# Two groups of a float32 graph product side by side, and a first half-tile rounded on VectorE

## The reference

```
h   = maximum((x - mean(x)) / sqrt(var(x) + 1e-5), 0)     # x: 4096 x 256, by row
agg = adj @ h                                             # adj: 4096 x 4096
out = x + maximum(agg @ W.T + b, 0)                       # W: 256 x 256
```

## Time and profile before

| What | Value |
|---|---|
| Time before | 380.95 us, median of 3 runs (380.69 to 380.96) |
| The profiled execution's own time | 380.8 us |
| Its span | 379.0 us |
| TensorE busy | 375.1 us, 99% of the span, 1651 matmuls |
| VectorE, ScalarE, GpSimd busy | 212.2, 181.8 and 50.1 us |
| Chain that ended last | TensorE 98% of it |
| Moved by DMA | 80.25 MB, mean 212 GB/s |

### The profile page before, as it was taken

The page is one execution under the profiler, slowest core; times in us unless marked ns, Lnnn a source line. Parts: engine busy times, 40 slices in busy tenths (PEclk is TensorE's granted clock), DMA queues, the critical chain, the costliest instruction groups (busy, mean ns, idle before and its releaser), DMA issues.

```text
span 379.0 us, 4516 instructions
## 1 busy us (share of the span) xinstructions
PE 375.1 (99%) x1651; PEld 308.1 (81%) x1651; DVE 212.2 (56%) x294; ACT 181.8 (48%) x228; POOL 50.1 (13%) x88
## 2 busy tenths in 40 slices
PE   8999999999999999999999999999999999999997
PEld 4888888888888888888888888888888888888885
DVE  5999988874744453535564544444464444444424
ACT  5888776764443434343643343433355243434341
POOL 5687732320010000000001000000000100000000
PEclk9999999999999999999999999999999999999999
DMA  7989877577659565655566856565656775555203
GB/s 263 369 301 304 275 256 258 185 235 256 210 186 317 174 215 178 208 177 209 176 206 207 294 178 209 178 205 184 201 189 195 256 242 195 187 202 185 92 2 111
DMA packets 22774, 80.25 MB, mean 212 GB/s; under 512 B 2496, under 2 KB 2880, under 8 KB 22752
## 3 DMA queue, kind: packets, MB, share of 16 engines
q1 hardware_dynamic: 19584, 68.30, 54.1%
q0 software_dynamic: 3168, 11.67, 8.6%
HBM read 75.76 MB, written 4.19 MB: 211 GB/s over the span
## 4 chain that ended last, share of the span: by engine, by line
PE 98%; DMA 1%; DVE 0%; ACT 0%; POOL 0%; issue 0%; POOLq 0%
PE bank L421 92%; PE bank L463 6%; DMA x_sb<-x_dram 1%; ACT adj_hi L346 0%; POOL rstd L204 0%; ACT h_sb L352 0%; DVE out_sb L320 0%; DVE stats L240 0%; DVE mean_var L245 0%; DVE var_eps L249 0%; POOLq L200 0%
## 5 line engine op out<-in xcount | busy, mean ns | idle before, releaser
L421 PE MATMUL bank<-adj_hi,h_sb 128*128 128x512 f32 x1024 | 254.3, 389 | 0.2 <-ACT adj_hi L346 0.2
L229 DVE TENSOR_TENSOR adj_lo<-adj_in,adj_hi 128x1024 fp32r<-128x1024 f32 x126 | 154.6, 1227 | 145.7 <-ACT adj_hi L342 145.5
L421 PEld LDWEIGHTS bank<-adj_hi,h_sb 128*128 128x128 f32 x1024 | 192.0, 188 | 40.5 <-issue 0.5
L342 ACT ACTIVATE adj_hi<-adj_in 128x1024 fp32r<-128x1024 f32 x126 | 133.5, 1060 | 176.7 <-PE bank L421 174.5
L421 PE MATMUL bank<-adj_lo,h_sb 128*128 128x512 f32 x512 | 137.5, 389 | 0.0
L421 PEld LDWEIGHTS bank<-adj_lo,h_sb 128*128 128x128 f32 x512 | 96.1, 188 | 20.0
L204 POOL TENSOR_TENSOR rstd<-var_eps,minus_half 128x1 f32<-128x1 f32 x32 | 30.5, 954 | 3.4 <-DVE var_eps L249 0.8
L221 POOL DMA_DIRECT2D out_t_dram<-out_sb x3 | 2.2, 726 | 211.0 <-DVE out_sb L320 211.0
L352 ACT ACTIVATE h_sb<-centred,rstd 128x256 fp32r<-128x256 f32 x32 | 16.0, 499 | 3.6 <-POOL rstd L204 3.2
L362 ACT ACTIVATE centred<-x_sb,neg_mean 128x256 f32<-128x256 f32 x31 | 15.5, 500 | 2.1 <-DVE neg_mean L264 1.9
L270 DVE SCALAR_TENSOR_TENSOR h_sb<-centred,rstd,h_sb 128x256 fp32r<-128x256 f32 x32 | 15.3, 477 | 1.0 <-ACT h_sb L352 1.0
(11 more groups left out here) (25 smaller groups left out, 42.7 us busy)
## 6 DMA issues: line engine op xcount, KB each, us to landing
adj_in<-adj_t_dram SPq DMA_DIRECT2D x126, 512.0 KB, 3.6
xt_sb<-x_t_dram POOLq DMA_DIRECT2D x4, 1024.0 KB, 7.4
x_sb<-x_dram POOLq DMA_DIRECT2D x7, 512.0 KB, 6.5
out_t_dram<-out_sb POOLq DMA_DIRECT2D x3, 1024.0 KB, 4.9
adj_in<-adj_t_dram SPq DMA_DIRECT2D x4, 256.0 KB, 4.8
out_t_dram<-out_sb SPq DMA_DIRECT2D x3, 256.0 KB, 2.0
x_sb<-x_dram POOLq DMA_DIRECT2D x3, 128.0 KB, 4.6
w_sb<-w_t_dram POOLq DMA_DIRECT2D x1, 256.0 KB, 6.0
```

Source lines behind the costliest of these rows:

```text
L229: nc.vector.tensor_tensor(adj_lo[:, k, :], adj_in[:, k, :], adj_hi[:, k, :].bitcast(fp32), ALU.subtract).then_inc(s_lo, 1)
L342: nc.scalar.activation(adj_hi[:, k, :], adj_in[:, k, :], ACT.Copy).then_inc(s_hi, 1)
L421: last = nc.tensor.matmul(bank(g, kb, c)[:], h_sb[:, t, hp, kb * P:(kb + 1) * P], adj_parts[ap][:, n % U, chunk(c)], start=(t == 0 and (hp ...
```

## The change

Three things change.

1. **Order of the units.** A table UNITS of (group, tile) pairs replaces the two nested loops, on all engines. Groups 0 and 1 take turns: (0, 0), (1, 0), (0, 1), (1, 1) and so on up to tile 23 of each (TILES - LAG = 24), so both use tile t of `h`; then come tiles 24 to 31 of group 0 and tiles 24 to 31 of group 1; groups 2 and 3 follow as before. The split and the output of a group stand 4 and 8 units behind that group's last unit: for group 0 ahead of units 60 and 64, for group 1 ahead of 68 and 72. The tiles of `h` are still made one per unit during the first 32 units, though TensorE now needs a new one only every second unit.
2. **The first chunk.** VectorE, not ScalarE, rounds chunk 0 of unit 0, with a `tensor_copy` from fp32 to fp32r. ScalarE waits for it before it rounds chunk 1. WARM_ON is 2 instead of 3. GpSimd issues the loads of x tiles 2 and 3 behind the first `root`, not at its beginning, and only then the 512 KB piece.
3. **The order within the first two units.** The low-`adj` product of chunk 0 is taken ahead of the low-`h` product of chunk 1, the one of chunk 1 at the very end. In the loop over the tiles of `h`, `h_rest` and `h_rounded` come one unit later than before, behind the `adj` work of the next unit.

```diff
-    WARM_ON = 3
+    WARM_ON = 2
+    LAG = 8
+    UNITS = [(g, t) for t in range(TILES - LAG) for g in range(2)]
+    UNITS += [(g, t) for g in range(2) for t in range(TILES - LAG, TILES)]
+    UNITS += [(g, t) for g in range(2, GROUPS) for t in range(TILES)]
...
+        SPLIT = {end_of(g) + SPLIT_AT: g for g in range(LAST)}
+        OUT = {end_of(g) + OUT_AT: g for g in range(LAST)}
...
         def _(pool):
-            for i in range(1, U):
-                load_x(pool, i)
+            load_x(pool, 1)
...
                 if t == 0:
-                    load_x(pool, U)
+                    for i in range(2, U + 1):
+                        load_x(pool, i)
...
+            def first_rounded():
+                dve.wait_ge(s_early[0][0], 16)
+                nc.vector.tensor_copy(adj_hi[:, 0, chunk(0)], adj_in[:, 0, chunk(0)]).then_inc(s_hi, 1)
...
             centre_first()
+            first_rounded()
             h_rest(0)
+            early_rest(0, 0)
+            early_rest(0, 1)
             moments(1)
             minus_mean(1)
-            early_rest(0, 0)
-            early_rest(0, 1)
-            moments(2)
-            minus_mean(2)
-            h_rest(1)
             early_rest(1, 0)
             early_rest(1, 1)
...
+            for n in range(EARLY, TILES + 1):
+                if n < TILES:
+                    moments(n)
+                    minus_mean(n)
+                adj_rest(n)
+                h_rest(n - 1)
...
             h_rounded(0)
-            early_rounded(0, 0)
+            act.wait_ge(s_hi, 1)
             early_rounded(0, 1)
+            early_rounded(1, 0)
             centre(1)
-            early_rounded(1, 0)
-            h_rounded(1)
             early_rounded(1, 1)
-            for t in range(EARLY, TILES):
-                centre(t)
-                adj_rounded(t)
-                h_rounded(t)
+            for n in range(EARLY, TILES + 1):
+                if n > EARLY:
+                    centre(n - 1)
+                adj_rounded(n)
+                h_rounded(n - 1)
...
+            def early_unit(n):
+                pe.wait_ge(s_hhi, 1)
+                pe.wait_ge(s_hi, made_chunk(n, 0))
+                add_up(n, [0], 0, 0)
+                pe.wait_ge(s_hlo, 1)
+                add_up(n, [0], 1, 0)
+                pe.wait_ge(s_hi, made_chunk(n, 1))
+                add_up(n, [1], 0, 0)
+                pe.wait_ge(s_lo, made_chunk(n, 0))
+                add_up(n, [0], 0, 1)
+                add_up(n, [1], 1, 0)
+                pe.wait_ge(s_lo, made_chunk(n, 1))
+                add_up(n, [1], 0, 1).then_inc(s_pe, 1)
```

More of the change, by code:

```diff
@@ L128, in x_piece, with end_of, made_chunk, made_unit @@
             return next(i for i, (a, b) in enumerate(X_PIECES) if a <= t < b)
-        def made_chunk(t, c):
-            return CHUNKS * t + c + 1
-        def made_tile(n):
+        def end_of(g):
+            return max(n for n, u in enumerate(UNITS) if u[0] == g) + 1
+        SPLIT = {end_of(g) + SPLIT_AT: g for g in range(LAST)}
+        OUT = {end_of(g) + OUT_AT: g for g in range(LAST)}
+        def made_chunk(n, c):
+            return CHUNKS * n + c + 1
+        def made_unit(n):
             return made_chunk(n, CHUNKS - 1) if n < EARLY else CHUNKS * EARLY + n - EARLY + 1
@@ L157, in _, with load_chunk @@
         def _(sp):
[L158 to L159 removed]
+            def load_chunk(n, c):
+                g, t = UNITS[n]
+                at = g * GW + c * BANK
+                sp.dma_start(adj_in[:, n, chunk(c)], adj_v[:, t, at:at + BANK]).then_inc(s_early[n][c], 16)
             def load_adj(n):
[L162 removed]
+                g, t = UNITS[n]
                 if n >= U:
[L164 to L165 removed]
+                    sp.wait_ge(s_hi, made_unit(n - U))
+                    sp.wait_ge(s_lo, made_unit(n - U))
                 sp.dma_start(adj_in[:, n % U, :], adj_v[:, t, g * GW:(g + 1) * GW]).then_inc(s_adj[n % U], 16)
@@ L173, in _ @@
             load_chunk(1, 1)
-            for n in range(EARLY, GROUPS * TILES):
+            for n in range(EARLY, len(UNITS)):
                 load_adj(n)
@@ L227, in adj_rest, with early_rest @@
                 k = n % U
-                dve.wait_ge(s_hi, made_tile(n))
+                dve.wait_ge(s_hi, made_unit(n))
                 nc.vector.tensor_tensor(adj_lo[:, k, :], adj_in[:, k, :], adj_hi[:, k, :].bitcast(fp32),
                                         ALU.subtract).then_inc(s_lo, 1)
[L232 to L235, removed]
+            def first_rounded():
+                dve.wait_ge(s_early[0][0], 16)
+                nc.vector.tensor_copy(adj_hi[:, 0, chunk(0)], adj_in[:, 0, chunk(0)]).then_inc(s_hi, 1)
+            def early_rest(n, c):
+                dve.wait_ge(s_hi, made_chunk(n, c))
+                nc.vector.tensor_tensor(adj_lo[:, n, chunk(c)], adj_in[:, n, chunk(c)],
+                                        adj_hi[:, n, chunk(c)].bitcast(fp32), ALU.subtract).then_inc(s_lo, 1)
             def moments(t):
@@ L322, in make_out @@
                                                    op0=ALU.max, op1=ALU.add).then_inc(s_sum, 1)
[L324 to L330, removed]
+            for n in range(TILES + 1, len(UNITS)):
+                if n in SPLIT:
+                    sums_rest(SPLIT[n])
+                if n in OUT:
+                    make_out(OUT[n])
+                adj_rest(n)
             sums_rest(LAST)
@@ L400, in _ @@
             act.wait_ge(s_b, 16)
[L401 to L407, removed]
+            for n in range(TILES + 1, len(UNITS)):
+                if n in SPLIT:
+                    sums_rounded(SPLIT[n])
+                if n in OUT:
+                    add_bias(OUT[n])
+                adj_rounded(n)
             add_bias(LAST)
@@ L425, in add_up, with sum_unit @@
                 return last
[L427 to L442, removed]
+            def early_unit(n):
[11 more added lines that the diff above has]
+                add_up(n, [1], 0, 1).then_inc(s_pe, 1)
+            def sum_unit(n, chunks, arrived):
+                g, t = UNITS[n]
                 for hp, ap in PASSES:
@@ L482, in _ @@
             warm_up(WARM_ON, BANK // 2)
[L483 to L489, removed]
+            for n in range(EARLY):
+                early_unit(n)
+            for n in range(EARLY, len(UNITS) - U):
+                g, t = UNITS[n]
+                if g >= 2 and t == 0:
                     pe.wait_ge(s_sum, (g - 1) * SUMS)
[L492 to L495, removed]
+                if n in SPLIT:
+                    pe.wait_ge(s_wlo, 1)
+                    w_product(SPLIT[n])
+                sum_unit(n, range(CHUNKS), False).then_inc(s_pe, 1)
             for c in range(CHUNKS):
-                for t in range(TILES - U, TILES):
-                    last = sum_tile(LAST, t, [c], c > 0)
+                for n in range(len(UNITS) - U, len(UNITS)):
+                    last = sum_unit(n, [c], c > 0)
                 last.then_inc(s_chunk, 1)
```

32 lines of the change are left out of this document (11 added, 21 removed).

## The result

The changed kernel takes 381.36 us (median of 22 runs, 380.85 to 382.18), the kernel before 380.92 beside it: ratio 1.0012 with a 95% interval of 1.0006 to 1.0017. That is 0.44 us slower. The forecast was 380.7 with a range to 381.3: a small gain became a small loss, and the time lies just outside the range. Timed once more (experiment 12), it was 381.54 against 380.82. The execution whose profile follows took 381.07 us, 0.27 more than the one profiled before the change (380.8); the rows explain this pair, and the medians lie 0.17 further apart.

What follows compares the result with a forecast made beforehand. TensorE was taken as the bound, standing still nowhere from 5.84 us to the tail. With -0.26 at the start and 0 elsewhere, the profiled 380.8 became 380.54; the median's 0.15 made it 380.7 us, range 380.25 to 381.3.

Steps and rivals of the forecast that it cites:

- Term 1: Start of TensorE: VectorE rounds the first chunk in 0.43, so the first real matmul moves from 5.84 to 5.58, -0.26 us.
- the upper bound of 0.68: VectorE's rounding of the first chunk: longest copy time considered, 0.68 us, which would make the start 0.0 to +0.05.
- Term 2: Chunk 1 in the first unit: landing 5.75, rounded 6.40, wanted by TensorE at 6.57, so no wait, 0.
- My margin of 0.15: Chunk 1 in the first unit: rounded at 6.40, said to be in time by 0.15 us for TensorE.
- Rival A: Start: gain swallowed at once, by a copy of 0.68 or a wait for chunk 1; 380.95 us, chance 0.25.
- Term 3: Unit 2: x tile 2 lands at 9.7, needed by 10.0, so VectorE's low part is in time, 0.
- rival B: Unit 2: late x tile 2 holds up VectorE's subtraction and TensorE; 383.1 us if it lands at 12.4; chance 0.11.

Runs made afterwards that it cites:

- experiment 12: The changed kernel and its version with x tiles 1 to 3 issued first, timed on one chip: 381.54 and 380.65 us, the kernel before 380.82.
- changed_again: The changed kernel without any edit, timed once more beside its version with early small loads: 381.54 us, ratio 1.0016 to the kernel before.
- rest_first: Changed kernel, with VectorE's subtraction of unit 2 ahead of the moments of x tile 2, load still late: 381.10 us, ratio 1.0002.
- x_early: Changed kernel, with GpSimd issuing the loads of x tiles 1 to 3 at its beginning, as before the change: 380.61 us, ratio 0.9991.
- x_early_again: Changed kernel with x tiles 1 to 3 issued first, timed again on the same chip as the changed kernel: 380.65 us, ratio 0.9999.
- cast_only: Kernel before the change, with only the first chunk rounded on VectorE and two short warm-ups: 380.87 us, ratio 0.9996.
- 1: The same run as x_early: changed kernel with the loads of x tiles 1 to 3 issued first: 380.61 us, ratio 0.9991.
- 9: The same run as x2_first: changed kernel with x tile 2 issued early, tile 3 still late: 380.62 us, ratio 0.9989.
- 7: Changed kernel, with VectorE waiting for x tile 2 right after rounding the first chunk: 389.06 us including the added wait.
- 8: Changed kernel, with SP issuing all whole loads only when x tile 2 has landed: 386.75 us including the added wait.
- 13: Changed kernel, with SP issuing unit 3 and all later loads only when x tile 2 has landed: 381.63 us including the added wait.
- units_only: Kernel before the change, with only the order of the units changed, splits and outputs following: 380.57 us, ratio 0.9988; again 380.62, ratio 0.9992.
- x2_first: Changed kernel, with x tile 2 issued with tile 1 at GpSimd's beginning, tile 3 still late: 380.62 us, ratio 0.9989.
- before_x_late: Kernel before the change, with only the loads of x tiles 2 and 3 moved behind GpSimd's first root: 384.65 us, ratio 1.0091.
- sequential: Changed kernel, with x tiles 1 to 3 issued first and the units in the old order, one group after another: 384.57 us, ratio 1.0092.

## Why the prediction was wrong

**The order of the units, forecast 0.** Nearly right. The steps are 0.2267 us through the turns of the groups, as computed. By itself the order gave 380.57 and 380.62, 0.45 and 0.27 under the kernel before beside it, with intervals that end at 0.9997 and 1.0001. A small gain is likely and its place is not shown: both executions profiled lay well above their medians. That the order lets some executions pass in which a landing comes late was only argued; this stays open.

**Term 1, the start, forecast -0.26, measured -0.43.** The first chunk had landed at 4.70 instead of 5.0. I had put its landing down to x tiles 2 and 3 being out of the way, and the runs don't bear this out: with the tiles late VectorE's rounding, which begins 0.02 behind the landing, stands at 4.72, 4.89 (changed_again) and 5.15 (rest_first), with the tiles early at 4.63 (x_early) and 4.82 (x_early_again). The landing varies by 0.5 us between executions, more than my range of 4.95 to 5.07, so part of the 0.43 is luck. The copy took 0.54 here, 0.43 or 0.44 in eight of the twelve traces that have it and 0.49 to 0.55 in the other four; what makes this difference the rows don't say. So 0.43, taken from L240, was nearer than the upper bound of 0.68. The Trainium skill, "VectorE: DVE Perf Modes", section "The perf-mode tier table", with its doubled rate for fp32 copies, agrees with the 0.43 for 512 elements, not with the 0.54 of this trace; a subtraction of as many took 0.69.

**Term 2, chunk 1, forecast 0, measured +0.18.** The landing was as forecast (ScalarE begins at 5.78; I had 5.75), but TensorE began 0.17 earlier than in my sum, and so it met the wait. My margin of 0.15 was also too wide, since it left out the 0.14 from a rounding to its matmul, which I had counted at the first chunk. Rival A was right as a mechanism, that the next chunk takes the gain back: in cast_only it is 0.29 of 0.40.

**Term 3, unit 2, forecast 0, measured +0.60. This is the step that failed.** The prediction said that x tile 2 must land by 10.0, took 5.2 us to landing from tile 3, and came to 9.7. It landed at 10.45, after 6.02 us. The threshold was right, and the mechanism stood there as rival B with its chain, from the tile by moments and subtraction to TensorE; its landing was put at 9.5, and I gave it 0.11. The 5.2 us belong to a load issued at 2.5, before the first whole load of `adj` was issued at 3.07; at 4.43 two of them stood ahead. The row of the same moment was at hand, 7.9 us for the 512 KB load, with the nearly empty software queue, one packet in 0.8 us; rival B took its whole wait to the first packet, about as it came (no packet before 8.0), then a quarter of its time for a quarter of its bytes, and did not allow for tiles 2 and 3 moving together: tile 3, issued at about 5.0, took 5.8 us and landed at about 10.8, 0.3 behind tile 2. The margin was 0.3 and the landing 0.75 later than the sum had it, which makes the 0.46 of the wait; the longer step behind it, 0.14, was in no term. Experiments 1, 9 and 12 put the whole loss against the kernel before on this tile, as far as medians tell; 7, 8 and 13 put its lateness on the hardware queue's backlog. Rival B's second reason, that GpSimd contends with VectorE there, was wrong: with VectorE idle the tile came no earlier.

The three measured terms, -0.43, +0.18 and +0.60, add up to +0.35, and the profiled executions differ by 0.27, their spans by 0.3. The medians differ by 0.44; what the typical execution loses beyond this pair is not in a trace.

**A threshold that is the same for the gain.** An earlier start moves every need of TensorE forward, so the same late tile costs more the better term 1 is: its need at unit 2 was 12.06, not 12.1, in spite of the wait for chunk 1. Start and tile are not two terms to be added with their own errors. My range treated them so and ended 0.06 too low.

**The best version.** Nothing here is under the kernel before by more than about 0.1%, and only units_only the first time and x2_first have an interval that ends below 1 (0.9997 and 0.9998): units_only (380.57 and 380.62), x_early (380.61 and 380.65), x2_first (380.62) all lie within 0.1 us of each other. What stands in the way of the earlier start is chunk 1's landing: in x_early_again the first six matmuls take 1.78 us to the next start instead of 1.44, and from there to 13.11 the steps are the usual ones.

## What to carry to other kernels

A small load moved behind other work is priced by what the other queues have already been given when it is issued, not by how long its neighbours took; take the row of the load that was issued at that very moment. When every engine runs in order, look for each wait that the late thing ends: taking the first one away (rest_first) showed the next, on another engine. Read a start time from more than one execution before giving it a cause: here the first chunk's landing varied by 0.5 us, as much as the whole effect. Where the main engine never stands, as here, the start is what there is to win, and the next input decides how much of it stays.

## What the runs showed of the hardware

- A load of 128 KB in the software queue, issued at about 4.4 us, landed after 3.3 and 4.6 us with no and one load of 512 KB ahead of it in the hardware queue, and after 6.0 to 7.1 with two. In the changed kernel not a packet of it moved for 2.8 us while the hardware queue held the engines at 99.9%. Earlier software packets had moved beside the hardware queue's: 12 of them beside 72 from 4.45 to 4.9 us. Which part of the path waits the rows don't say.
- Behind a short wait TensorE's first steps are longer: four matmuls took 1.05 us to the next start in the changed kernel and 1.03 in rest_first (15.30 to 16.33) instead of 0.91.
- A stand of TensorE of 3.0 us in before_x_late was followed by a granted clock of 0.50 (1.2 GHz) from 12.2 to 15.5 us, in the execution profiled; by their mean clock it happened in three of six executions and cost about 1.6 us. In sequential, with a stand of 2.48 us, one of two executions has the lower mean clock. Behind the wait of 0.46 us in the changed kernel the granted clock stayed at 1.00.
